# Reordering a three-stage decoder layer on one core: the opening, the end of self attention, and where two quads of outputs are scaled

## The reference

```python
Q, K, V, dl = (projections of x)                    # 16 heads, 64 wide (V: 16), 12 levels
dt  = softplus(x @ Wdt.T + dt_bias); g = -exp(A_log) * dt
Lam = softplus(Lp * dl);             cg = cumsum(g, axis=1)
decay  = exp(cg[t] - cg[s]) for s <= t
scores = Q K^T * S**-0.5 * decay * Lam[level(t, s)]  # level: size class of t XOR s
o = (scores @ V) @ Wout.T + x ; layer norm           # self attention
x = layer norm(x + o)
x = layer norm(x + softmax(q k^T / 4) v @ Wo + bo)   # cross attention to 1024 context rows
x = layer norm(x + experts(x))                       # 32 experts, each takes its 8 best tokens
```

## Time and profile before

| | |
|---|---|
| median of 3 runs | 1792.65 us (1788.92 to 1797.26) |
| the profiled execution | 1791.35 us, its span 1789.6 us |
| mean granted TensorE clock | 0.965 of 2.4 GHz |
| self attention | 0 to some 629 us |
| cross attention | some 629 to 1632 us; a batch in the loop takes 121 us |
| experts and combination | some 1632 to 1790 us |

### The profile page before, as it was taken

One profiled execution on the slowest core, in us unless ns is written; L12 is line 12 of the kernel. 1 busy time (PEld: TensorE's weight loads), 2 busy tenths in 40 slices (PEclk: granted clock), 3 DMA queues, 4 the chain that ended last, 5 costly groups with the idle time before them and its releaser, 6 DMA issues. The chain is left out here.

```text
span 1789.6 us, 48945 instructions
## 1 busy us (share of the span) xinstructions
PE 1659.9 (93%) x19942; PEld 802.0 (45%) x19942; DVE 1277.5 (71%) x2414; ACT 814.5 (46%) x981; POOL 587.1 (33%) x926
## 2 busy tenths in 40 slices
PE   6899999999999789999999999999999999898557
PEld 3566666666666423343343333433433434234224
DVE  5667677677774577888878889788788888842004
ACT  2334343343342215656556656565466565561103
POOL 3535545554552454316034043060250420000002
PEclk8999999999999859999999999999999999998879
DMA  7000000000000130211111202211112121438995
GB/s 258 3 4 3 3 3 3 3 3 3 3 33 3 36 93 25 86 57 44 59 57 48 92 32 78 67 44 59 57 44 81 36 74 60 192 116 344 420 419 217
DMA packets 66062, 146.04 MB, mean 82 GB/s; under 512 B 12320, under 2 KB 36128, under 8 KB 58176
## 3 DMA queue, kind: packets, MB, share of 16 engines
q1 hardware_dynamic: 65296, 142.34, 21.9%
q10 hardware_dynamic: 560, 0.72, 0.2%
HBM read 92.43 MB, written 7.86 MB: 56 GB/s over the span
## 5 line engine op out<-in xcount | busy, mean ns | idle before, releaser
L1716 DVE TENSOR_REDUCE mx<-cpsV 128x1 f32<-128x512 f32 x1024 | 652.9, 685 | 114.2 <-PE cpsV L1428 93.7
L1625 ACT ACTIVATE w<-cpsA 128x1024 f32<-128x1024 f32 x512 | 496.3, 1021 | 253.6 <-PE cpsA L1489 248.5
L1428 PE MATMUL cpsV<-w 96*128 96x512 bf16 x1024 | 332.5, 394 | 29.0 <-DVE mx L1716 16.1
L1489 PE MATMUL cpsA<-w 99*128 99x512 bf16 x1024 | 272.3, 381 | 5.8 <-ACT w L1603 3.4
L1450 PE MATMUL cacc<-w 128*32 128x512 f32 x2048 | 273.3, 606 | 0.4 <-ACT w L1625 0.4
L472 PE MATMUL psA<-w 128*128 128x512 f32 x512 | 257.9, 627 | 8.3 <-DVE WT L1105 3.5
L1428 PEld LDWEIGHTS cpsV<-w 96*128 96x128 bf16 x1024 | 85.3, 98 | 308.8 <-DVE mx L1716 227.5
L1683 POOL TENSOR_TENSOR crstd<-cmv,mhalf 128x4 f32<-128x4 f32 x8 | 8.2, 1019 | 579.9 <-DVE cmv L1791 579.9
L772 ACT COPY w<-psA 128x1024 f32<-128x1024 f32 x64 | 64.8, 1013 | 233.4 <-PE psA L472 233.4
L1489 PEld LDWEIGHTS cpsA<-w 99*128 99x128 bf16 x1024 | 93.8, 97 | 135.3 <-ACT w L1625 10.9
L890 POOL TENSOR_TENSOR VP<-V,VPF 128x128 f32<-128x128 f32 (+2 forms) x256 | 130.1, 540 | 44.4 <-PE psA L485 39.8
(11 more groups left out here) (232 smaller groups left out, 2202.3 us busy)
## 6 DMA issues: line engine op xcount, KB each, us to landing
w<-in_w SPq DMA_DIRECT2D x56, 1024.0 KB, 16.4
w<-w SPq DMA_DIRECT2D x189, 128.0 KB, 2.3
w<-w SPq DMA_DIRECT2D x189, 64.0 KB, 2.0
w<-in_ctxT SPq DMA_DIRECT2D x8, 1024.0 KB, 5.2
w<-in_xT SPq DMA_DIRECT2D x8, 512.0 KB, 6.4
x_tok<-in_x SPq DMA_DIRECT2D x8, 512.0 KB, 9.7
w<-in_w SPq DMA_DIRECT2D x8, 512.0 KB, 17.2
out_y<-w SPq DMA_DIRECT2D x16, 256.0 KB, 2.3
```

What stands on the lines that cost most here:

```text
L1428: nc.tensor.matmul(out, Qst[q // 2][0:ROWS, hh, g * P:(g + 1) * P], Kst[q // 2][0:ROWS, hh, half * BANK:(half + 1) * BANK], start=True, st ...
L1489: last = nc.tensor.matmul(out[:, n * T:(n + 1) * T], Kst[q // 2][0:ROWS + 3, hh, chunk * P:(chunk + 1) * P], Qst[q // 2][0:ROWS + 3, hh, : ...
L1625: nc.scalar.activation(Pr[:, (2 * s + pp) % 4, :], src, ACT.Exp, scale=CA_SCALE).then_inc(act_evac, 1)
L1716: nc.vector.tensor_reduce(mx[:, q % 2, row, k % 2:k % 2 + 1], full(m[k]), AX_X, ALU.max).then_inc(dve_evac, 1)
```

## The change

It has four parts, and two functions are cut in two for it.

1. Opening: DVE does seven of the nine coefficients of `lam`, then the bias and -|z| of dt, then the other two coefficients and `level_factors`, and only then the polynomial of dt. `level_factors` used to follow `spread_sums`.
2. End of self attention: x1T goes from the start of iteration 0 to its end, the queries from the end of iteration 0 to the end of iteration 1, and the first half of the keys from iteration 2 to iteration 3, behind the output projection. ACT copies in the same order.
3. Quad 0 is scaled in step 9 instead of step 12; it is still transposed back in step 12.
4. Quad 2 (the third): DVE takes the reciprocals in step 25 into a buffer of their own, and POOL multiplies, behind the last `parts` of the batch and ahead of its copy of x for the next. In step 1 DVE only waits for POOL and transposes back.

```diff
-def log1p_poly(eng, acc, u):
+def log1p_poly(eng, acc, u, first=0, last=None):
...
-CROSS_JOBS = {0: ["cq"], 2: [("ck", 0)], 3: [("ck", 1), "cv"]}
+CROSS_JOBS = {0: ["x1T"], 1: ["cq"], 3: [("ck", 0), ("ck", 1), "cv"]}
...
+BEFORE_STEPS = 7
...
-                    if sec == "tail" and i == 0:
-                        cross_tokens()
...
                     if sec == "tail":
                         if i == 0:
+                            cross_tokens()
+                        if i == 1:
                             cross_queries()
-                        if i == 2:
+                        if i == 3:
                             pe.wait_ge(ca.ctx_loaded, 16)
                             cross_keys(0)
-                        if i == 3:
                             cross_keys(1)
...
-                    log1p_poly(nc.vector, lam[:].rearrange("p g h l -> p (g h l)"), ul[:])
+                    lamf = lam[:].rearrange("p g h l -> p (g h l)")
+                    log1p_poly(nc.vector, lamf, ul[:], 0, BEFORE_STEPS)
                     dve.wait_ge(dt_loaded, 16 * 3)
+                    time_steps()
+                    log1p_poly(nc.vector, lamf, ul[:], BEFORE_STEPS)
+                    level_factors()
                     decay_sums()
                     dve.wait_ge(cgt_ready, 1)
                     spread_sums()
-                    level_factors()
                     block_factors()
...
+                    t = byq[0][:, :, 0:BLK:2]
+                    pool.wait_ge(rec_ready, b + 1)
+                    nc.gpsimd.tensor_tensor(t, t, rec2[:].unsqueeze(2).broadcast_to([P, KT * 2, HD]), ALU.mult
+                                            ).then_inc(third_scaled, 1)
...
                         if sec != "tail":
-                            outputs(b - 1, 2)
+                            dve.wait_ge(third_scaled, b)
+                            turn_outputs(b - 1, 2)
                         outputs(b - 1, 3)
...
                             if now:
-                                outputs(b, 0)
+                                turn_outputs(b, 0)
...
+                    if now and s == SCALE_OUTPUTS:
+                        scale_outputs(b, 0)
...
+                    if nxt and s == RECIPROCALS:
+                        nc.vector.reciprocal(rec2[:], byq[0][:, :, 1]).then_inc(rec_ready, 1)
```

More of the change, by code:

```diff
@@ L87, in negated_abs @@
     return nc.vector.scalar_tensor_tensor(out=out, in0=x, scalar=-1.0, in1=x, op0=ALU.mult, op1=ALU.min)
-def log1p_poly(eng, acc, u):
+def log1p_poly(eng, acc, u, first=0, last=None):
     c = _log1p_coefficients()
-    eng.tensor_scalar(acc, u, c[0], None, ALU.mult)
-    eng.drain()
-    for ck in c[1:]:
+    if first == 0:
+        eng.tensor_scalar(acc, u, c[0], None, ALU.mult)
+        eng.drain()
+    for ck in c[max(first, 1):last]:
         eng.scalar_tensor_tensor(out=acc, in0=acc, scalar=ck, in1=u, op0=ALU.add, op1=ALU.mult)
@@ L139 @@
 PROJECT_K, X2T, COPY_X2, GATE, GATE_MAX, GATE_EXP, TOP8, TOP8_T, PICK, PICK_T = (7, 12), 9, 10, 10, 12, 14, 20, 21, 28, 29
-PROJECT_V0, LAST_OUTPUTS = 20, 27
+PROJECT_V0, LAST_OUTPUTS, SCALE_OUTPUTS, RECIPROCALS = 20, 27, 9, 25
 BEHIND_JOBS = (PROJECT_V1 + 1, PROJECT_K[0] + 1)
@@ L286, in sa_jobs @@
         a += [("state", i)] * (sa_pair(section, i, 2) is not None)
-        a += ["x1T"] * (i == 0 and section == "tail")
         a += [("qk", i)] * now
@@ L768, in body @@
                                        ).then_inc(act_evac, 1)
-                    if sec == "tail" and i == 0:
-                        nc.scalar.copy(ca.x1T[:].rearrange("p k t -> p (k t)"), full("x1T")).then_inc(act_evac, 1)
                     if now:
@@ L802, in body @@
                     if sec == "tail" and i == 0:
+                        nc.scalar.copy(ca.x1T[:].rearrange("p k t -> p (k t)"), full("x1T")).then_inc(act_evac, 1)
+                    if sec == "tail" and i == 1:
                         cross_whole("cq", 0)
@@ L1063, in output_factors, with time_steps @@
                     dve.drain().then_inc(lam_used, 1)
-                def decay_sums():
+                def time_steps():
                     dve.wait_ge(dt_full, 1)
@@ L1071, in decay_sums @@
                     negated_abs(nc, dt_g, dt_z).then_inc(dt_abs, 1)
+                def decay_sums():
                     dve.wait_ge(dt_exp, 1)
@@ L1248, in cross_attention @@
         byd = [sb(f"byd_{n}", [P, T]) for n in range(2)]
-        rec = sb("rec", [P, KT * 2])
+        rec, rec2 = sb("rec", [P, KT * 2]), sb("rec2", [P, KT * 2])
         o2 = sb("o2", [P, G, D])
@@ L1269, in cross_attention @@
         var, rstd_ready = sem("ca_var"), sem("ca_rstd")
+        rec_ready, third_scaled = sem("ca_rec"), sem("ca_third_scaled")
         bo_added, x2_ready, x2_copied, xs_ready = sem("ca_bo_added"), sem("ca_x2"), sem("ca_x2_copied"), sem("ca_xs")
@@ L1739, in max_rows, with outputs @@
                         dve.nop().then_inc(dve_evac, 1)
+                def outputs(bb, q):
+                    scale_outputs(bb, q)
+                    turn_outputs(bb, q)
                 def take_outputs(bb, q):
@@ L1745, in take_outputs, with scale_outputs @@
                     dve.drain()
-                def outputs(bb, q):
+                def scale_outputs(bb, q):
                     t = byq[q % 2]
@@ L1754, in outputs, with turn_outputs @@
                     dve.drain()
+                def turn_outputs(bb, q):
+                    t = byq[q % 2]
                     dve.wait_ge(o_moved[q % 2], bb * 32 + (q // 2 + 1) * 16)
```

1 line of the change is left out of this document (added).

## The result

Before: 1790.23 us median (1788.15 to 1798.78, 13 runs). After: 1782.46 us median (1777.70 to 1788.11, 13 runs). The ratio is 0.9936 with a 95% interval of [0.9921, 0.9951], a gain of 9 to 14 us; the medians are 7.8 us apart and the means 10.5, so its size is known to a few us only. The forecast was 1782. The profiled execution of after took 1788.11 us, the slowest of its thirteen, at a span of 1786.4 us. So the two profiles are only 3.2 us apart, and the first question to them is what in a profile is the kernel's and what that one execution's.

The account below looks back on a forecast made before the run. PE, busy 93% of the span, bounds the loop; at self attention's ends engines wait in turn. 1.0 + 5.4 + 4.3 = 10.7 us, taken from the median 1792.65, gives 1782; its own range 1778 to 1787, for all 1775 to 1790.

Parts of the forecast that it names:

- The opening: Start of self attention: 1.0 us gained, bounds a loss of 0.5 and a gain of 2.5.
- The loss of 0.2 us: Opening: L1046 starts at 51.25 instead of 51.05 because DVE now waits for ACT, 0.2 us longer.
- this mechanism: Opening: PE waits 2.2 us instead of 3.46; if its clock stays up, 2.5 us return, taken as 1.2.
- The end: End of self attention: the reordered work on PE and ACT gives 5.4 us, bounds 3.5 and 7.0.
- The chain of steps: End of self attention: far at 593.4, projection at 601.0, DVE's statistics ending at 609.2 instead of 614.69.
- first rival: End of self attention gains 3.5 instead of 5.4 us, the opening nothing: 7.6 in all, 1785; chance 0.18.
- late instructions: End of self attention: 2 us in which PE's instructions came late near 589, assumed to stay where they are.
- lower bound: End of self attention: a gain of 3.5 us if all queries run at the lower clock.
- Quad 0: Cross attention, steps 9 and 12: loop 4.0, last batch 0.8, first batch costs 0.5; sum 4.3 us, bounds 1 and 6.
- second limit of step 12: Rival: ACT's copy or the next buffer holds PE, 0.1 instead of 0.66 us remains per batch, 1785.4; chance 0.14.
- The rival with a multiplication held for all four of POOL's instructions: Step 9: DVE waits 2.3 us for POOL's group, PE loses 14 us over seven batches, 1795.5; chance 0.06.
- Quad 2: Third quad's multiplication on POOL, steps 25 and 1 of cross attention: worth nothing, until POOL is 17 us late.

Follow-up runs that it names:

- e5: Kernel before with only the first half of the keys moved behind the output projection, x1T and queries left in place; ratio 0.9996 [0.9980, 1.0013].
- e7: Kernel after with dt's chain and cg put ahead of the rest of the level polynomial and level_factors; ratio 0.9942 [0.9923, 0.9962].
- e8: Kernel after with quad 0 scaled in step 12 again in the first batch of cross attention only; ratio 0.9931 [0.9908, 0.9955].
- e9: e8 plus 24 unread identity transposes in each of PE's waits for the weights of groups 3 to 6, expert stage; ratio 0.9946 [0.9929, 0.9962].
- e1: Kernel before with the new opening alone; ratio 0.9998 [0.9984, 1.0013].
- e10: e9 plus filler transposes in the opening's wait for VP and ahead of far at the end of self attention; ratio 0.9949 [0.9935, 0.9963].
- e2: Kernel before with the new order at the end of self attention alone; ratio 0.9977 [0.9963, 0.9991].
- e4: Kernel before with only quad 2 (the third) multiplied by POOL; ratio 0.9992 [0.9973, 1.0012].
- e6: Kernel before with only the queries moved to the end of iteration 1, x1T at the start and keys as before; ratio 0.9997 [0.9977, 1.0018].
- e3: Kernel before with quad 0 scaled in step 9 alone; ratio 0.9970 [0.9957, 0.9984].

## Why the prediction was right, and where its terms were not

**The forecast**, 1782 against 1782.5, was right in what it summed, but that it came so near is luck: two errors cancel. One term was 2.4 us too large (the end of self attention, 5.4 for 3.0), and the sum was taken from a start 2.4 us too high: 1792.65, the median of three runs of before, where thirteen have 1790.23. From that median the same 10.7 us would have given 1779.5, which is still within its range. The 10.7 us came apart as follows.

**The opening: 1.0 us, measured about 1.5.** Each step on DVE came out: `cg` 34.62 (34.5 forecast), L1046 at 51.28 (51.25) behind a wait for ACT. After's DVE began 0.23 us later, though (14.67 against 14.44), and from there L1046 starts as early as before, 36.61 us in both; it then takes 1.43 us instead of 1.27. The loss of 0.2 us is there in clean form: e5, the old order without a lower clock behind WT, has 48.31, and the new order 48.47 to 48.49 in five profiles, with or without a lower clock before WT, and with filler. The new opening is bound by DVE's chain to WT. The gain is the clock: in the old order it was lower behind WT's wait of 1.8 to 3.5 us for 3.4 to 5.9 us in five of six profiles, at a cost of 1.6 to 2.5 us; in the new order it was up again by WT's start in five profiles, and 0.6 us behind it in e7. The mean over the old openings is 50.0, against 48.5. The prediction had this mechanism and took half of its gain, but not how it would come about. It expected PE to wait 2.2 us for WT with the clock staying up. In after PE doesn't wait there at all: the clock had fallen before, at 49.6 us, so that the four matmuls ahead of WT took 3.17 us (1.98 at the upper clock) and filled the wait, and it was up again from 53.0 us. So it was in e8 and e9, whose waits were 0.51 and 0.28 us; in e1 and e10 it didn't fall, and PE waited 1.71 and 1.80 us. Nor was the lower clock of before all behind the wait: it began at 52.8 us, 1.4 us ahead of the wait's end. Since e5 has the same in the old order, the order makes this likely and doesn't force it.

**The end: 5.4 us, measured 2.8 with the clock up, 3.0 as a mean.** The chain of steps was right (e2), but this term was mis-sized, by its first sentence: "the queries took PE from 590.99 for 5.40 us, partly at the lower clock". The prediction took the old order with that lower clock, which was that execution's, and the new one with "3.6 us, plus one at the lower clock", so a piece of the execution's clock was counted as the order's gain. Like with like: with the clock up during the queries the old order took 39.2 and 39.6 us, the new one 36.1, 37.0, 36.8 and 36.5, 2.8 less on average. With it down the old took 41.7 and 42.4, the new 40.7 and 39.4, 2.0 less. The clock was down in two of four old and in two of six new profiles (e10 with its filler among them).

These 2.8 us aren't the order's alone either. In both old profiles with the queries at the upper clock it fell for 3.4 us behind them, at 597.7 in e4 and 596.8 in e1, over the transposes of the sums and the first keys. PE's timeline in e4:

```profile
597.80 1.94 PE L465 MATMUL psA<-ident,w 128*128 128x128 f32 x8 [2.39 <-DVEq L1126]
...
599.53 4.36 PE L601 MATMUL psA<-w,w 128*128 128x512 f32 x8
```

In e2 the same transposes take 1.04, and eight such matmuls take 3.60 at the upper clock, so I estimate 1.7 us of lower clock here, and as much in e1; little more than 1 us of the 2.8 is left for the order at an equal clock. Between the last WT and the long period at the start of cross attention the clock was lower somewhere in all four old profiles and in both halves, and in three of the six new ones (after, e7, e10). That may mean that the new order gains mostly by the clock; so few profiles suggest it and don't show it. The prediction's first rival, that the chain at the end gains less, with 3.5 us for the sake of the clock, was nearer than its forecast.

A second thing moves the stage: PE pauses in or near the `near` of pair 6 (before: [1.61 <-issue]; the prediction's "late instructions") for 0.88 us in e1, e4, e5 and e6, 1.61 and 1.88 in before and e3, and 1.36 to 1.90 in after, e2, e7, e8 and e9. The prediction kept it in its forecast, and it did stay; what causes it is open.

Over all ten profiles the means are 40.7 and 37.7. The lower bound given was 3.5, for "all queries at the lower clock"; after's own profile gained only 1.0 against before's, with nearly all of the eight at that clock (6.54 us). Whether the keys must move as well as the queries, e5 and e6 leave open.

**Quad 0: 4.3 us, measured about 3.8.** From step 9 of the loop's first batch to step 9 of the last, the six profiles with quad 0 scaled in step 12 took 718.6 us as a mean and the six with step 9 took 714.8, so the loop gave 3.8 us for the 4.0 forecast (before's and after's own profiles: 718.8 and 714.8); the last batch 0.8 for 0.8 (after's own 2.5 is one execution in which its clock stayed up); the first batch cost 0.77 for 0.5. The second limit of step 12 wasn't there: ACT's 0.25 us remain, and the output matmuls start 0.97 us behind the scores. The rival with a multiplication held for all four of POOL's instructions was out by a wide margin: 0.38 us each.

**Quad 2: nothing**, as forecast (e4).

The measured terms add up to 1.5 + 3.0 + 3.8 + 0.8 - 0.8 = 8.3 us. The medians say 7.8, the means 10.5 and the interval 9 to 14. The difference of some us isn't resolved: it may lie in the times' own spread, or in the clock of stages like "rest", which one profile of each kernel cannot average.

## What to carry to other kernels

A stage's length in one profile is the order's length plus where the clock fell; before a term is taken from it, see which instructions ran at which level, and compare like with like, in this kernel by the time of eight identical matmuls. Where several engines wait for each other in turn, the gain of a filler or of an earlier chain ends at the next engine: 1.2 us of faster matmuls and 3.9 us of an earlier `cg` moved nothing here. In a loop bound by one engine, a piece of work of another engine is worth just the wait that it causes, and it costs nothing in the step in which that other engine idles.

## What the runs showed of the hardware

The lower clock behind the same wait differs from execution to execution of the same code: behind WT's wait of 1.8 to 3.5 us it lasted 0, 3.4 or 5.6 to 5.9 us, and the same eight matmuls of 512 columns took 3.70, 5.40 or 6.54 us. The periods in the opening and at the end of self attention were 3.4, 6.8 or 10.2 us long. The period of some 41 us at the start of cross attention (44 in e6) was there in all twelve profiles.

The stage behind the last projection took 181 to 182 us in nine profiles, 184.3 in one and 187.6 in two. In these two, after and e2, each of the last two groups of eight adds of x took 3.78 us instead of before's 1.99: 3.6 us of the 6 are the clock in the last 20 us. In after that is over half of the 5.7 us by which its profiled execution, its slowest, lies above its median; the rest of them isn't accounted for.
